# One table of order in place of a greedy scheduler: 3411 steps of a Mamba-like block with a ternary feed-forward

## What is computed

```python
x = x + mamba(layernorm(x));  x = x + ffn(layernorm(x))

def mamba(u):                         # 8 heads of 64, state 16, causal conv of 4 taps
    z0, x0, xBC, dt = split(u @ W_in.T)
    dt = softplus(dt + dt_bias);  A = -exp(A_log)
    x, B, C = split(silu(causal_conv(xBC) + conv_b))
    h_t = exp(dt_t * A) * h_(t-1) + dt_t * x_t * B_t
    y_t = C_t . h_t + D * x_t
    y = layernorm(y) * gamma + beta
    y = sigmoid(y @ W_gate.T + b_gate) * y
    return concat(silu(z0) * x0, y) @ W_out.T

def ffn(x):                           # weights rounded to -1, 0, 1 by their mean magnitude
    h = gelu(x @ tern(W_fc).T)
    return (layernorm(h) * ln_w + ln_b) @ tern(W_proj).T
```

## Time and profile before

| | us |
|---|---|
| median of 3 runs | 1275.65 |
| lowest, highest | 1275.33, 1280.67 |
| the profiled execution | 1281.52 |
| its span | 1279.6 |
| PE busy in it | 1154.4 (90%), 8534 matmuls |
| DVE busy | 994.8 (78%) |
| ACT busy | 960.4 (75%) |
| POOL busy | 393.4 (31%) |
| mean granted TensorE clock | 0.961 of full speed |

### The profile page before, as it was taken

One profiled execution on the slowest core, in us unless ns is written; L12 is line 12 of the kernel. 1 busy time (PEld: TensorE's weight loads), 2 busy tenths in 40 slices (PEclk: granted clock), 3 DMA queues, 4 the chain that ended last, 5 costly groups with the idle time before them and its releaser, 6 DMA issues.

```text
span 1279.6 us, 22535 instructions
## 1 busy us (share of the span) xinstructions
PE 1154.4 (90%) x8534; PEld 736.7 (58%) x8534; DVE 994.8 (78%) x1958; ACT 960.4 (75%) x1662; POOL 393.4 (31%) x500
## 2 busy tenths in 40 slices
PE   4577889999999999999999999999998999989885
PEld 1354565647575665657575666656565574747453
DVE  5889786878978798979888897979787696666443
ACT  5847466787979797887879797887877867676744
POOL 1112314152423324142524324252522314232420
PEclk9878899999999999999999999999998999999896
DMA  4720103242423433242423333232253203222443
GB/s 138 202 64 9 34 10 67 34 108 41 94 59 71 80 56 95 42 100 51 92 51 87 71 67 76 51 92 57 52 99 72 54 18 75 50 67 50 82 83 82
DMA packets 238971, 89.10 MB, mean 70 GB/s; under 512 B 207760, under 2 KB 235152, under 8 KB 238864
## 3 DMA queue, kind: packets, MB, share of 16 engines
q1 hardware_dynamic: 238864, 87.67, 32.1%
HBM read 24.32 MB, written 8.39 MB: 26 GB/s over the span
## 4 chain that ended last, share of the span: by engine, by line
PE 59%; ACT 17%; DVE 13%; DMA 5%; issue 4%; POOL 2%; SPq 0%; ACTq 0%; DVEq 0%
PE bank L166 29%; PE bank L140 29%; ACT h L141 3%; ACT L161 3%; DMA hT<-hb 2%; DVE cv L144 2%; DVE EM L144 2%; DVE hb L142 2%; ACT yT L141 2%; ACT hb L141 2%; ACT cv L141 2%; ACT yhl L141 1%; DVE tg L144 1%; POOL caty L142 1%; DVE hn L144 1%
## 5 line engine op out<-in xcount | busy, mean ns | idle before, releaser
L166 PE MATMUL bank<-xnT,win 128*128 128x512 f16 (+1 forms) x1040 | 264.7, 386 | 23.4 <-DMA xnT<-hb 19.1
L144 DVE SCALAR_TENSOR_TENSOR cv<-bank,cws,cv 128x510 f32<-128x510 f32 (+5 forms) x240 | 178.3, 744 | 13.5 <-ACT cv L141 3.0
L166 PE MATMUL bank<-yhl,wg 128*128 128x512 f16 x704 | 169.5, 391 | 10.8 <-DVE yhl L142 10.8
L166 PEld LDWEIGHTS bank<-xnT,win 128*128 128x128 f16 (+1 forms) x1040 | 100.2, 102 | 133.3 <-issue 30.6
L140 PE MATMUL bank<-wpj,hT 128*128 128x256 f16 x1040 | 133.8, 285 | 26.5 <-DMA hT<-hb 23.9
L140 PE MATMUL bank<-wfc,x3T 128*128 128x512 f16 x512 | 132.6, 387 | 8.4 <-DVE dec L145 3.6
L161 ACT ACT_TABLE_LOAD x105 | 134.7, 1283 | 1.9
L140 PEld LDWEIGHTS bank<-wpj,hT 128*128 128x128 f16 x1040 | 103.7, 102 | 53.6 <-ACT hb L141 12.2
L141 ACT ACTIVATE h<-bank,rs 128x512 f32<-128x512 f32 x128 | 87.4, 683 | 62.2 <-PE bank L140 61.2
L166 PEld LDWEIGHTS bank<-yhl,wg 128*128 128x128 f16 x704 | 69.8, 100 | 99.3 <-issue 13.7
L142 POOL TENSOR_TENSOR caty<-tg,caty 128x512 f16<-128x512 f32 x64 | 82.6, 1291 | 114.2 <-ACT caty L141 114.2
(11 more groups left out here) (137 smaller groups left out, 2298.5 us busy)
## 6 DMA issues: line engine op xcount, KB each, us to landing
x<-in_x SPq DMA_DIRECT2D x32, 512.0 KB, 4.2
out_y<-x SPq DMA_DIRECT2D x15, 512.0 KB, 3.0
crep<-cv SPq DMA_DIRECT2D x128, 32.0 KB, 2.0
hT<-hb SPq DMA_TRANSPOSE x128, 3.2
segR<-segL SPq DMA_DIRECT2D x64, 6.0 KB
caty<-in_wg SPq DMA_DIRECT2D x1, 1024.0 KB, 6.0
x<-in_wout SPq DMA_DIRECT2D x1, 1024.0 KB, 9.3
hT<-in_wfc SPq DMA_DIRECT2D x1, 1024.0 KB, 11.4
```

Of the source, the lines that this page charges most:

```text
L144: "scalar_tensor_tensor": lambda e: e.scalar_tensor_tensor(*args, **kw),
L166: self.queue.append(lambda e: e.matmul(*args, **kw))
```

## The change

`PLAN`, `PERIOD`, `SHIFT`, the guesses, the `Token` with its time, `start_of` and the greedy loop go. In their place stands `ORDER`, a string with two characters for each of 3411 steps: a letter for the task, a hexadecimal digit for the block. A step does what it did before, with the same tiles and waits; its generator is resumed when the table names it. `take` now takes the bank that was given back first in the order of the table. The cut diff:

```diff
-SWITCH = 1.3
-PLAN = {
...
-}
-PERIOD = 76.36
-SHIFT = (0.0, -0.0, 0.0, 0.0, 0.0, 0.0, 0.0, 0.0, 0.0, 0.0, 0.0, 0.0, 0.0, -10.8, -2.4, 7.8)
-AHEAD = 5
-EPS = 0.1
+STEPS = dict(zip("abcdefghijklmnopqrstu", (
+    "ln1", "conv", "silu", "dt_chain", "inputs", "decay", "states", "mix", "yout", "gate",
+    "skip", "out", "turn3", "ln3", "fc", "proj", "loads", "win", "wgate", "wout", "wffn")))
+ORDER = (
+    "a0a0a0a0a0a0q0r0r0b0f0b0r0k0a1b0k0b0b0b0b0b0b0c0c0b0b0k0k0a1d0a1a1b0a1a1q0b0b0b0d0d0b0b0d0d0k0k0k0b0b1k0"
...
         def take():
-            return free.pop(min(range(len(free)), key=lambda k: when(free[k][1])))
+            return free.pop(0)
...
-                yield Need(PE, ("yT", i), banks=1)
+                yield Need(("yT", i), banks=1)
...
-        while live or at < NBLK:
-            while at < NBLK and (at < AHEAD or ("done", at - AHEAD) in dn):
-                for task in TASKS:
-                    spawn(task.__name__, at, task(at))
-                at += 1
-            starts = [(start_of(task.need), task) for task in live]
-            first = min(t for t, _ in starts if t is not None)
-            task = min((q for t, q in starts if t is not None and t <= first + EPS), key=lambda q: q.due)
-            task.move()
-            if task.need is None:
-                live.remove(task)
+        for letter, digit in zip(ORDER[::2], ORDER[1::2]):
+            name, i = STEPS[letter], int(digit, 16)
+            if (name, i) not in live:
+                gen = TASKS[name](i) if name in TASKS else PREP[name]()
+                live[name, i] = gen, next(gen)
+            gen, need = live[name, i]
+            check(need)
+            live[name, i] = gen, next(gen, None)
```

More of the change, by code:

```diff
@@ L99, in wait @@
             self.queue.append(lambda e, sem=sem, value=value: e.wait_ge(sem, value))
[L101 to L131, removed]
     def do(self, waits, name, *args, **kw):
@@ L325, in old, with check @@
             return dn[name, n] if n >= 0 else None
[L327 to L335, removed]
-            if need.banks:
-                if len(free) < need.banks:
-                    return None
-                t = max(t, sorted(when(f) for _, f in free)[need.banks - 1])
-            if need.lock and need.lock in locked:
-                return None
-            return t
+        def check(need):
+            assert all(k in dn or (not isinstance(k[1], tuple) and k[1] < 0) for k in need.keys), need.keys
+            assert len(free) >= need.banks and need.lock not in locked
         x_v = x_d.rearrange("b (i c p) d -> (b i) p c d", c=NCH, p=P)
@@ L423, in prep_out @@
             for half, s in ((0, SW), (1, SW / 2)):
-                yield Need(A, ("two", 0))
+                yield Need(("two", 0))
                 k0 = 4 * half
@@ L508, in hilo_T @@
             dn[hb0] = [t_hi, v]
-            yield Need(SP, ("split", done))
+            yield Need(("split", done))
             t_lo = SP.dma([v] + ready, sems[1], 16 * count, dst[1], stage[:, 1, :], transpose=True)
@@ L701, in decay @@
             dn["ahl_read", i] = m
-            yield Need(A, ("ahl_read", i), func="Exp")
+            yield Need(("ahl_read", i))
             dn["es", i] = A.do([m, old("be", i - 1)], "activation", esuf[:, :, :].rearrange("p c e -> p (c e)"),
@@ L762, in mix @@
                 at, hs, es = 4 * i + n, slice(4 * half, 4 * half + 4), slice(4 * (n % 2), 4 * (n % 2) + 4)
-                yield Need(PE, ("R", i), ("own", at - 2), banks=2, func="Exp")
+                yield Need(("R", i), ("own", at - 2), banks=2)
                 seg = []
@@ L771, in mix @@
                 dn["seg", at] = [m for _, _, m in seg]
-                yield Need(A, ("seg", at), func="Exp")
+                yield Need(("seg", at))
                 exps = []
@@ L790, in yout @@
                 js = (2 * half, 2 * half + 1)
[L791 removed]
+                yield Need(("EM", 4 * i + 2 * half), ("ce", i), ("S_done", i), banks=2)
                 hold = {j: take() for j in js}
@@ L946, in fc @@
                 for n in range(2):
-                    yield Need(PE, ("x3T", i), ("wq", 0), ("h_read", at - 2), banks=1, func="Gelu")
+                    yield Need(("x3T", i), ("wq", 0), ("h_read", at - 2), banks=1)
                     b, f = take()
@@ L1003, in proj @@
             dn["done", i] = True
-        TASKS = (ln1, conv, silu, dt_chain, inputs, decay, states, mix, yout, gate, skip, out, turn3, ln3, fc, proj)
-        live = []
-        class Task:
-            def __init__(self, name, block, gen):
-                self.plan = PLAN[name] if name in PLAN else (0.0,)
-                self.base = block * PERIOD + SHIFT[block]
-                self.gen = gen
-                self.step = -1
-                self.move()
-            def move(self):
-                self.step += 1
-                self.need = next(self.gen, None)
-                self.due = self.base + self.plan[min(self.step, len(self.plan) - 1)]
@@ L1023, in spawn @@
-        def spawn(name, block, gen):
-            task = Task(name, block, gen)
-            if task.need is not None:
-                live.append(task)
-        spawn("loads", 0, loads())
-        for name, task in (("win", prep_win), ("wgate", prep_gate), ("wout", prep_out), ("wffn", prep_ffn)):
-            spawn(name, 0, task())
-        at = 0
-        while live or at < NBLK:
-            while at < NBLK and (at < AHEAD or ("done", at - AHEAD) in dn):
-                for task in TASKS:
-                    spawn(task.__name__, at, task(at))
-                at += 1
-            starts = [(start_of(task.need), task) for task in live]
-            first = min(t for t, _ in starts if t is not None)
-            task = min((q for t, q in starts if t is not None and t <= first + EPS), key=lambda q: q.due)
-            task.move()
-            if task.need is None:
-                live.remove(task)
+        TASKS = {f.__name__: f for f in (ln1, conv, silu, dt_chain, inputs, decay, states, mix, yout, gate, skip, out, turn3, ln3,
+                                            fc, proj)}
@@ new lines, in build @@
+        PREP = {"loads": loads, "win": prep_win, "wgate": prep_gate, "wout": prep_out, "wffn": prep_ffn}
+        live = {}
+        for letter, digit in zip(ORDER[::2], ORDER[1::2]):
[6 more added lines that the diff above has]
+            live[name, i] = gen, next(gen, None)
@@ L1043, in build @@
+        assert all(need is None for _, need in live.values())
         SP.wait(dn["x2_read", NBLK - 2], dn["x2_read", NBLK - 1])
```

253 lines of the change are left out of this document (149 added, 104 removed), and 4 rows, old and new, of the table PLAN.

## The result

| | before | after |
|---|---|---|
| median | 1275.49 (4 runs) | 1204.98 (4 runs) |
| lowest, highest | 1270.81, 1280.67 | 1203.58, 1206.41 |
| ratio, 95% interval | | 0.9446 [0.9407, 0.9485] |
| the profiled execution | 1281.52 | 1206.41 |
| its span | 1279.6 | 1204.3 |

The change gives 70.5 us in the medians and 75.3 us between the two profiled spans; 40 were forecast. Of the 75.3 us, 48.5 are idle time of PE and 26.8 its busy time. The 8534 matmuls are the same, so I count the fall of busy time as the clock's. Busy time times what is missing from a clock of 1.00 is 45.0 us before and 25.9 after, so the granted clock shows 19 of the 26.8; for the rest it is not shown.

The account below looks back on a forecast made before the run. PE bounds the middle; lead-in and end lose time to PE idling and a lower clock, with DVE busy in the lead-in. Gains of 14 + 9 + 4 + 9 + 4 = 40 us off 1275.65 give 1236 us, range 1217 to 1259.

Parts of the forecast that it names:

- The lead-in, 14 us: Up to 176 us: 7.5 us from earlier ACT work, 3.5 from `ahl` waits, 3 other idle; bounds 5 and 20.
- this lies beside the ACT chain just counted and costs nothing in my sum: Near 50 us: `segR` copies behind 4.5 MB of loads make block 0's `mix` up to 3 us late, priced at nothing.
- Gate 1 to 11, 9 us: Forecast for 176 to 936 us: repeated PE waits worth 13.5 us go, a third given back; bounds 0 and 14.
- 936 to 1164 us, 4 us: Late blocks: a quarter of PE's 15.8 us idle time goes, 4 us; bounds 0 and 8.
- The end, 9 us: Last block: third chunk's `fc` moved ahead 5.5 us, `proj` and `fc` moves 2.7, DVE split 0.8; bounds 5 and 12.
- The clock, 4 us: Whole kernel: less PE idle time means fewer half-speed stretches, 4 us of 37; bounds 0 and 12.
- Table loads and banks, nothing: Three more ACT table loads, 3.8 us, hidden in ACT's idle time; taking banks by table order changes nothing.
- those for right: Magnitude-sum wait below 2 us, PE idle near 26 us from 24 to 176, last `out` to end 6 us less, others.
- those for wrong: Repeated `EM` wait, `segR` wait over 3 us near 50 us, DVE 95% busy in lead-in, or block period still 71 us.
- New small waits in the middle: Rival: new waits replace the middle's old ones, only the ends gain, 23 us: 1253 us; chance 0.17.
- any repeated one for `EM`: Slower rival: late recurrence makes PE wait for `EM` in each half block, about 1290 us; chance 0.05.
- PE is relieved more: Rival: lead-in 20 us, middle 14, late blocks 8, end 12, clock 12, together 66: 1210 us; under 1220 has chance 0.06.

Follow-up runs that it names:

- the split version: New kernel with the loads of W_out and the vectors issued behind block 0's small `segR` copies: 1201.76 us, ratio 0.9431; repeated, 1199.49 us, 0.9397.

## Why the prediction was wrong, point by point

**What bounds the kernel: right.** PE does the same work in either, the three regimes are where they were, and the time went where PE stopped waiting or ran at a higher clock.

**The lead-in, 14 us: too high, with a wrong step inside.** The loads moved to 35 us, PE's wait of 8.7 us for the magnitude sums is gone, the waits for `ahl` fell from 14.6 to 4.9 us. Idle time fell by 9.8 us only, because of the step "this lies beside the ACT chain just counted and costs nothing in my sum": the wait for `segR` is 6.3 us, twice its bound of 3. That it does lie on the path is shown by the split version, 3 to 6 us faster. The landing itself was forecast well, at 51 to 52 us, and PE went on at 51.73. The error was to hold it against the time at which PE came to the copies in the kernel before, 48.8 us. By the step just ahead of it PE comes earlier, here at 45.4, so the wait is 6.3 us and not 3: one gain of the sum was not carried into the next price. That issuing a load can itself hold the queue, 5.13 us here, was missed as well. In total the piece gained 15.5 us, but 5.7 of them are busy time, which the sum had priced under the clock; that 14 and 15.5 lie close is luck.

**Gate 1 to 11, 9 us: right.** 10.9 us of idle time, and the waits for `caty` and `yhl` are gone from 328 to 755 us. That work between `gate` and `out` hides the wait for `caty` is shown, since taking all of it out in nine blocks costs 86.7 us. How much of the 10.9 us the few steps give that the new order added there is not shown by itself. `hT` is the one that stayed, 1.7 against 2.1 us.

**936 to 1164 us, 4 us: the first step that failed.** It read "idle 15.8 us, of many kinds, one of them 2.4 us for EM. I take a quarter". The real number is 21.6 us of idle time in blocks 11 to 14 (19 to 21 against the three other executions of the old order). Two errors. The stretch by time held 15.8 us, but the last gates before 936 us and those behind 1164 us belong to the same regime; cut at gates 11 and 15, it is 23.8 us. And "of many kinds" was read as hard to remove, where the same argument as for the middle held: I never looked at what the table puts into these gaps. Its upper bound was 8, half of the idle time, with no reason for the half. With the share taken for the middle, two thirds, the step would have given 16 of 23.8.

**The end, 9 us: right in kind, a little high.** Idle time fell by 6.3 us. The third chunk's Gelu follows with 0.20 us idle in place of 5.50; one wait for `hT` of 4.74 us stayed. Of the chain's 5.5 us the run with the old order of `fc` and `proj` gives back 3 to 4.

**The clock, 4 us: the second step that failed, and the larger.** It came to 26.8 us of busy time, 19 of them shown by the granted clock. The text had the right rule, each half-speed stretch follows idle time, and even worked out that a third of the 37 us should go, 12.5; then it took 4, as "part of the stretches lies where DVE binds anyway". No row stood behind that cut. The upper bound, 12, was lower than its own product. Uncut, and with the 48.5 us of idle time that did go, the same step gives 17 us, close to the 19; the 8 us beyond them no step of the text held. What the runs put in its place is a price per wait: 3.35 us busy on 5.85 idle in one gap, 27.7 on 59.0 in nine, 26.8 on 48.5 in the whole change, so 0.47 to 0.57 us of busy time for each us of idle time.

**Table loads and banks, nothing: right.** The banks by 3 us on the bad side.

**The signs.** Of those for right, the wait for the magnitude sums is gone, and from the last `out` to the end it takes 7 us less, 36.1 against 43.1. PE's idle time from 24 to 176 us is 31.6 us and not 26. Of those for wrong, the wait for `segR` of over 3 us near 50 us came.

**The rivals.** New small waits in the middle did not come, nor any repeated one for `EM`. "PE is relieved more" names the time that came, at 1205 beyond its 1210, and had 0.06, but its make-up did not: it gave the lead-in 20 us, the middle 14 and the late blocks 8, where 9.8, 10.9 and 21.6 were found. Its failure and the forecast's are one: forecast and bound both left late blocks and clock low.

The account closes: the two failed terms were too low by 17.6 and 22.8 us; lead-in, middle and end (9.8 us of idle time against 14, 10.9 against 9, 6.3 against 9) were together too high by 5.0. That makes 35.4, but for rounding the difference between 40 forecast and 75.3 found in the spans.

## What to carry to other kernels

Cut two traces at the same event of the bounding engine, not at the same time, and price every regime with the same question, what the new order puts into each gap; idle time "of many kinds" is not idle time that stays. A wait of several microseconds of TensorE in the midst of dense work cost its length and half as much again here, so the clock belongs to each wait's price and not into a separate small term. When one part of a change brings an engine earlier to a place, price the next wait from the new time. Before moving small copies behind big loads, ask when they land and how long the issue of the loads holds the queue; a second queue did not help here, and letting the loads that no one waits for stand behind the copies did.

## What the runs showed of the hardware that I had not expected

- The price of a single wait: 4.46 us ahead of `out` came with nearly double times in the next groups, 1.47 to 2.72 us and 1.36 to 2.55 us, and nothing in eight later blocks made it good.
- Issuing takes its engine's time: the same load (`lnwb`, 512 KB) took 5.13 us to issue directly behind four loads of 1 MB, and 0.57 us behind one of them and the four small copies. On ACT four copies of 6 KB took 3.62 us of issue, in which it did no other work.
- Copies of 24 KB in all, put on a queue of their own beside 4.5 MB of loads, were moved in 108 packets over 5 us, and the last one no earlier than when they stood behind the loads in one queue: at 51.1 us, against 50 to 51.
- Two executions with the same first 1498 steps reached gate 0 at 117.8 and 120.4 us; a difference of 2.6 us in a lead-in, from one profile each, tells nothing.
